# Another order of side work in the first tile of a fused group-norm, mixture-of-experts convolution

## The chip, the cores and the metric

The kernel runs on one core of a Trainium2 chip. The metric is the device time of one execution in microseconds (us), the median of several runs. The lower the better.

## The reference

The input is a batch of 32 images with 384 channels of 28 x 28 pixels (784 per image). Each image is group-normalised (32 groups), passes a layer of 4 experts, and is added to the input:

```python
def _L0_conv_ref(x, gate_w, gate_b, w1, b1, w2, b2):
    scores = jax.nn.softmax(x_flat @ gate_w + gate_b, -1)
    top_v, top_i = jax.lax.top_k(scores, K)          # K = 2
    top_w = jax.nn.softmax(top_v, -1)
    wmap = top_w.T.reshape(K, b, h, w)
    present = (top_i[:, :, None] == jnp.arange(e)[None, None, :]).any(0)
    coef = jnp.einsum('ke,kbhw->ebhw', present.astype(x.dtype), wmap)
    hdn = jax.nn.relu(jnp.einsum('bchw,edc->ebdhw', x, w1) + b1[:, None, :, None, None])
    y = jnp.einsum('ebdhw,eod->ebohw', hdn, w2) + b2[:, None, :, None, None]
    out = jnp.einsum('ebohw,ebhw->bohw', y, coef)
    return out
...
x = x + _L0_conv_ref(_gn(x), ...)
```

Every pixel goes through all four experts (384 to 384 to 384). The gate only weights them: `present` says which experts are first or second choice anywhere in the batch, and `coef` weights each expert at each pixel.

## The kernel before, in words

**Tiling.** The 32 x 784 pixels are cut into 49 tiles of 512. A tile has 12 chunks, one for each expert and each 128 of its 384 hidden units; chunk q runs from 0 to 587. Three chunks (one expert of one tile) are a unit u. Each product is made of three matmuls in a reduced fp32 format, from a rounded part (`_hi`) and a remainder (`_lo`) of both operands. One chunk of the first layer (`mm1`, to `z_ps`) is nine matmuls of 128x512, and one chunk of the second layer (`mm2`, to `y_ps`) is nine too. This text calls either of them a group of nine.

**The pipeline of a chunk.** TensorE (PE) makes z. VectorE (DVE) adds the bias and multiplies by the coefficient (`scale(q)`, output `hid`). ScalarE (ACT) takes the rounded part (`split_h_hi(q)`, `h_hi`). DVE makes the remainder (`split_h_lo(q)`, `h_lo`). PE multiplies by the second weights. `z_ps` has four buffers, so `mm1` of chunk q waits for `scale(q-4)`. PE's order is `mm1` of unit u+1, then `mm2` of unit u.

**Order.** Each engine's program is one list in the order of the code, with semaphores between engines; there is no scheduler. DVE's loop runs over q, and in iteration q it does `scale(q+1)`, then `split_h_lo(q)`, then the side work that is written for this q. If `scale(q+1)` waits, `split_h_lo(q)` stands behind it.

**Side work.** For each image: statistics (`stats` in two halves, `group_stats`), a power on GpSimd (POOL), `norm_columns`, `normalise` in two halves. For each tile: its rounded part and remainder in one or two pieces (`split_x_hi` on ACT, `split_x_lo` on DVE). For each image the gate: `gate_product` on PE (to `g_ps`), `gate_copy` on ACT, `gate_logits` on DVE, `gate_exp` on ACT, `gate_top2` and `gate_gap` on DVE, `gate_gap_exp` on ACT, `gate_weights` and `gate_coefs` on DVE (output `wrow`). SyncE's queue (SP) stores `wrow` to `rows_dram` (`rows_out`) and loads it back over all partitions as `rows` (`rows_in`). `scale` of the first chunk of a tile waits for its `rows`. Tile 0 lies in image 0; tile 1 needs images 0 and 1, so chunk 12 (the first of tile 1) waits for the gate of image 1. For each tile `add_bias` prepares the residual in `res`, and `add_product`, two chunks into the next tile, adds `y_ps` to it and frees `y_ps` for the next tile's `mm2`.

**The start.** Before the loop, PE makes the first eight chunks with `mm1_early` (chunks 0 to 2, 3 to 5, and 6 and 7), ACT rounds the weights (`weight_hi`) and empties the first four z with `relu_early` into `early`, and DVE makes weight remainders (`weight_lo`; `weight_lo(0, 3)` is that of the first layer's fourth expert, used from chunk 9 on). `sum_counts` is the small PE product that sums the counts of the experts' picks. `biases` makes `bias01` and `bias_gap` from 9 tiny DVE instructions; `add_bias` and `add_product` use them.

Of the kernel before, what the change touches and what calls it, by code (L numbers as in the profile page):

```python
# [9 lines left out]
NK = HID // P  # L10
# [16 lines left out]
EARLY = 4  # L27
# [37 lines left out]
def conv_moe(nc, x, gate_w, gate_b, w1, b1, w2, b2, out):  # L65
# [7 lines left out]
    with ctx:  # L73
# [141 lines left out]
        main = Sems("")  # L215
# [171 lines left out]
                                    hi[:, e].rearrange("p j d -> p (j d)").bitcast(f32),  # L387
                                    ALU.subtract).then_inc(ready, 1)

        def mm1_early(pe, u, chunks, terms):  # L390


            for i, term in enumerate(terms):
                if term == "hl":
                    pe.wait_ge(main.xlo_ready, 1)
                if term == "lh":
                    pe.wait_ge(w1lo_ready, u + 1)
                if term == "hh":
                    pe.wait_ge(main.xhi_ready, 1)
                    pe.wait_ge(whi_ready[0], u + 1)  # L400
                for k in chunks:
                    q = NK * u + k
                    if i == 0 and q >= ZB:
                        pe.wait_ge(early_done, q - ZB + 1)
                    ks = slice(k * P, (k + 1) * P)
                    for j in range(NJ):
                        w = (w1_hi, w1_lo)[term[0] == "l"][:, u, j, ks]
                        x = (x_hi, x_lo)[term[1] == "l"][:, 0, j]
                        ins = nc.tensor.matmul(z_ps[:, q % ZB], w, x, start=(i == 0 and j == 0),
                                               stop=(i == 2 and j == NJ - 1))  # L410
                    if i == 2:
                        ins.then_inc(z_ready, 1)

# [134 lines left out]
        def _(dve):  # L548
            lk = Links(dve, dve_step, 0)
# [87 lines left out]
            for q in range(CHUNKS):  # L637
# [3 lines left out]
                if q < CHUNKS - 1:  # L641
                    scale(dve, q + 1)
                split_h_lo(dve, q)
                if r == 4:
                    add_bias(dve, t, lk)
                if q == 0:
                    stats(dve, main, 1, 1, 0, lk)
                if q == 1:
                    stats(dve, main, 1, 1, 1, lk)
                    weight_lo(dve, 0, 3)  # L650
                if q == 2:
                    group_stats(dve, main, 1, lk)
                    biases(lk)
                if q == 3:
                    split_x_lo(dve, 1, 0)
                    norm_columns(dve, main, 1, lk)
                    normalise(dve, main, 1, 1, 0, HALF)
                if q == 4:
                    normalise(dve, main, 1, 1, HALF, PIX)
                if q == 5:  # L660
                    split_x_lo(dve, 1, 1)
                if q == 7:
                    gate_logits(dve, main, 1, lk)
# [3 lines left out]
                if q == 9:  # L667
                    gate_weights(dve, 1, lk)
                    gate_coefs(lk, wrow_ready)
                for n, off in preparing(q):  # L670
                    if off == 0:
                        stats(dve, main, n // SLOTS + (n % SLOTS > 0), n % SLOTS, 0, lk)
                    if off == 1:
                        stats(dve, main, n // SLOTS + (n % SLOTS > 0), n % SLOTS, 1, lk)
                        group_stats(dve, main, n, lk)
                    if off == 3:
                        norm_columns(dve, main, n, lk)
                        normalise(dve, main, n, n % SLOTS, 0, HALF)
                    if off == 4:
                        normalise(dve, main, n, n % SLOTS, HALF, PIX)  # L680
                    if off == 10:
                        gate_logits(dve, main, n, lk)
                    if off == 11:
                        gate_top2(dve, main, n, lk)
                        gate_gap(dve)
                    if off == 13:
                        gate_weights(dve, n, lk)
                        gate_coefs(lk, wrow_ready)
# [6 lines left out]
        def _(act):  # L695
# [12 lines left out]
            act.wait_ge(small_loaded, 48)  # L708
            gate_gap_exp(act, 0)
            weight_hi(1, 0)  # L710
            weight_hi(1, 1)
            relu_early(act, 0)
            weight_hi(1, 2)
            relu_early(act, 1)
            weight_hi(1, 3)
            for q in range(2, EARLY):
                relu_early(act, q)
            split_x_hi(act, 1, 0)
            act.wait_ge(flag_ready, 1)
            flag = act.value_load(missing[0:1, 0:1], min_val=0, max_val=1)  # L720
# [6 lines left out]
            for q in range(CHUNKS):  # L727
                t, r = divmod(q, TILE_CHUNKS)
                split_h_hi(act, q)
                if q == 4:  # L730
                    split_x_hi(act, 1, 1)
                if q == 6:
                    gate_copy(act, main, 1)
                if q == 7:
                    gate_exp(act, main, 1)
                if q == 8:
                    gate_gap_exp(act, 1)
# [87 lines left out]
        def _(pe):  # L825
# [3 lines left out]
                nc.tensor.matmul(g_ps[:, 0:P], ones[:, :], ones[:, :], start=True, stop=True)  # L829
            gate_product(pe, main, 0, 0)  # L830
            mm1_early(pe, 0, range(NK), ("hh", "lh", "hl"))
            sum_counts(pe, main)
            mm1_early(pe, 1, range(NK), ("hh", "hl", "lh"))
            mm1_early(pe, 2, range(2), ("hh", "hl", "lh"))
            pe.wait_ge(flag_ready, 1)
            flag = pe.value_load(missing[0:1, 0:1], min_val=0, max_val=1)
# [3 lines left out]
                sum_counts(pe, scan)  # L840

            for u in range(UNITS):
                if u == 2:
                    gate_product(pe, main, 1, 1)
                for n in range(2, B):
                    if NK * u == TILE_CHUNKS * first_tile(n) - LEAD + 8:
                        gate_product(pe, main, n, n % SLOTS)
                if 0 < u < UNITS - 1:
                    mm1(pe, u + 1, chunks=range(2 if u == 1 else 0, NK))
                mm2(pe, u)  # L850


# [24 lines left out]
```

## Time and profile before

| | |
|---|---|
| median of 3 runs | 2474.2 us (2473.63 to 2474.5) |
| profiled execution | 2474.33 us |
| its span | 2472.5 us |
| PE busy | 2451.0 us, 99% of the span |
| DVE busy | 1414.0 us, 57% |
| ACT busy | 465.4 us, 19% |
| chain that ended last | PE 98%, DVE 2% |

The span is the time between the first and the last recorded instruction; 1.8 us of the profiled execution's time lie outside it. Busy time of PE counts overlapping matmuls once, so idle time can be read as gaps. In a timeline row the columns are the start, the busy time, the engine, the line, the operation with its output and inputs, the count, and in square brackets the idle time of the engine before it with what ended it. A 128x512 matmul has a busy time of 0.39 us, but its successor starts 0.23 us after it, since matmuls are pipelined.

### The profile page before, as it was taken

Reading aid. Unit: us, or ns where it says so; the run is one execution under the profiler, and the core shown is the slowest. Engines: PE = TensorE matmul, PEld = TensorE weight load, DVE = VectorE, ACT = ScalarE, POOL = GpSimd, SP = SyncE. Lnnn points to the kernel's source line nnn. Section 1 sums busy time; section 2 is a strip of 40 time slices with the busy share of each in tenths; the row PEclk is TensorE's granted clock in tenths of the full one; section 3 lists DMA queues with packets and bytes.
Section 4 is the critical chain, followed back from the end, with each engine's and each line's share of the span. In section 5 each row is a group of like instructions: output and inputs, shape, how many; then the busy total and the mean of one; then the engine's idle time right before and its main releaser. Section 6 shows DMA issues by size and latency. Waiting matters only on the chain.

```text
span 2472.5 us, 27781 instructions
## 1 busy us (share of the span) xinstructions
PE 2451.0 (99%) x11372; PEld 2010.6 (81%) x11372; DVE 1414.0 (57%) x2952; ACT 465.4 (19%) x777; POOL 52.6 (2%) x36
## 2 busy tenths in 40 slices
PE   7999999999999999999999999999999999999999
PEld 5888888888888888888888888888888888888887
DVE  8656546556565565645564565546556564555443
ACT  3121111112111111111111121112112111121111
POOL 0000000000000000000000000000000000000000
PEclk9999999999999999999999999999999999999999
DMA  5223121321222113221322123121211222113110
GB/s 184 90 70 114 49 89 58 102 71 49 89 81 81 67 49 108 75 68 47 101 83 68 67 72 112 49 89 67 96 67 49 90 94 68 67 51 106 56 47 26
DMA packets 127520, 189.58 MB, mean 77 GB/s; under 512 B 16032, under 2 KB 80800, under 8 KB 127392
## 3 DMA queue, kind: packets, MB, share of 16 engines
q1 hardware_dynamic: 127392, 187.80, 22.4%
q8 instruction: 89, 1.46, 0.2%
q14 instruction: 39, 0.32, 0.0%
HBM read 146.03 MB, written 41.75 MB: 76 GB/s over the span
## 4 chain that ended last, share of the span: by engine, by line
PE 98%; DVE 2%; DMA 0%; issue 0%; POOL 0%; SPq 0%; ACT 0%; DVEq 0%; POOLq 0%
PE z_ps L430 16%; PE y_ps L449 16%; PE y_ps L451 16%; PE y_ps L450 16%; PE z_ps L432 16%; PE z_ps L431 16%; PE g_ps L300 1%; DVE w_lo L386 0%; DMA x_raw<-in_x 0%; DVE h_lo L488 0%; DVE x_raw L278 0%; DVE st L245 0%; DMA rows_dram<-wrow 0%; DVE hid L477 0%; DVE hid L474 0%
## 5 line engine op out<-in xcount | busy, mean ns | idle before, releaser
L477 DVE SCALAR_TENSOR_TENSOR hid<-z_ps,b_sb,rows 128x512 f32<-128x512 f32 x584 | 436.7, 748 | 901.9 <-PE z_ps L432 894.5
L449 PE MATMUL y_ps<-h_lo,w_hi 128*128 128x512 f32 x1764 | 687.2, 390 | 4.3 <-DVE h_lo L488 4.3
L451 PE MATMUL y_ps<-h_hi,w_hi 128*128 128x512 f32 x1764 | 686.9, 389 | 0.0
L450 PE MATMUL y_ps<-h_hi,w_lo 128*128 128x512 f32 x1764 | 686.8, 389 | 0.0
L430 PE MATMUL z_ps<-x_lo,w_hi 128*128 128x512 f32 x1740 | 680.9, 391 | 2.2 <-DVE hid L477 2.2
L432 PE MATMUL z_ps<-x_hi,w_hi 128*128 128x512 f32 x1740 | 677.4, 389 | 0.0
L431 PE MATMUL z_ps<-x_hi,w_lo 128*128 128x512 f32 x1740 | 676.8, 389 | 0.0
L484 ACT ACTIVATE h_hi<-hid 128x512 fp32r<-128x512 f32 x588 | 368.5, 631 | 1562.3 <-DVE hid L477 1553.4
L488 DVE SCALAR_TENSOR_TENSOR h_lo<-hid,h_hi 128x512 fp32r<-128x512 f32 x588 | 401.1, 682 | 8.3 <-ACT h_hi L484 7.1
L449 PEld LDWEIGHTS y_ps<-h_lo,w_hi 128*128 128x128 f32 x1764 | 331.5, 188 | 74.8 <-DVE h_lo L488 5.3
L430 PEld LDWEIGHTS z_ps<-x_lo,w_hi 128*128 128x128 f32 x1740 | 326.6, 188 | 78.8 <-issue 12.3
L451 PEld LDWEIGHTS y_ps<-h_hi,w_hi 128*128 128x128 f32 x1764 | 331.5, 188 | 68.8
L450 PEld LDWEIGHTS y_ps<-h_hi,w_lo 128*128 128x128 f32 x1764 | 331.5, 188 | 68.7
L432 PEld LDWEIGHTS z_ps<-x_hi,w_hi 128*128 128x128 f32 x1740 | 326.7, 188 | 68.5
L431 PEld LDWEIGHTS z_ps<-x_hi,w_lo 128*128 128x128 f32 x1740 | 326.7, 188 | 67.1
L506 DVE SCALAR_TENSOR_TENSOR res<-y_ps,bias,res 128x512 f32<-128x512 f32 x147 | 101.1, 743 | 111.5 <-PE y_ps L451 111.5
L495 DVE SCALAR_TENSOR_TENSOR res<-rows,bias_gap,res 128x512 f32<-128x512 f32 x147 | 101.5, 746 | 0.0
L267 POOL TENSOR_TENSOR rstd<-gvar_eps,minus_half 128x8 f32<-128x8 f32 x32 | 52.4, 1638 | 2221.8 <-DVE gvar_eps L262 2221.8
L245 DVE BATCH_NORM_STATS2 st<-x_raw 128x6 f32<-128x392 f32 x186 | 92.4, 552 | 0.0
L292 DVE TENSOR_TENSOR x_lo<-x_raw,x_hi 128x1536 fp32r<-128x1536 f32 (+31 forms) x80 | 90.3, 1129 | 0.0
L286 ACT CAST x_hi<-x_raw 128x1536 fp32r<-128x1536 f32 (+31 forms) x80 | 77.1, 964 | 5.0 <-DVE x_raw L278 5.0
L278 DVE TENSOR_SCALAR x_raw<-x_raw,norm 128x1176 f32<-128x1176 f32 (+1 forms) x64 | 69.9, 1093 | 1.2
(88 smaller groups left out, 374.4 us busy)
## 6 DMA issues: line engine op xcount, KB each, us to landing
rows<-rows_dram SPq DMA_DIRECT2D x48, 1280.0 KB, 6.1
x_raw<-in_x SPq DMA_DIRECT2D x62, 588.0 KB, 5.9
res<-in_x SPq DMA_DIRECT2D x18, 768.0 KB, 5.6
out<-res SPq DMA_DIRECT2D x17, 768.0 KB, 4.3
rows_dram<-wrow SPq DMA_DIRECT2D x32, 98.0 KB
w_in<-in_w SPq DMA_DIRECT2D x3, 576.0 KB, 10.2
res<-in_x SPq DMA_DIRECT2D x2, 744.0 KB, 4.9
out<-res SPq DMA_DIRECT2D x2, 744.0 KB, 4.1
```

The lines of the kernel that those rows point to most:

```text
L245: ins = nc.vector.bn_stats(st6[:, HALVES * j + h], x_raw[:, q, j, half(h)])
L430: nc.tensor.matmul(z, w1_hi[:, e, j, ks], lo, start=(j == 0), stop=False)
L431: nc.tensor.matmul(z, w1_lo[:, e, j, ks], hi, start=False, stop=False)
L432: ins = nc.tensor.matmul(z, w1_hi[:, e, j, ks], hi, start=False, stop=(j == NJ - 1))
L449: nc.tensor.matmul(y, w2_hi[:, e, k, ms], h_lo[:, slot], start=first, stop=False)
L450: nc.tensor.matmul(y, w2_lo[:, e, k, ms], h_hi[:, slot], start=False, stop=False)
L451: ins = nc.tensor.matmul(y, w2_hi[:, e, k, ms], h_hi[:, slot], start=False, stop=last)
L477: nc.vector.scalar_tensor_tensor(hid[:, q % HIDS], z_ps[:, q % ZB], b1_sb[:, e, k:k + 1], coef, ALU.add, ALU.mult).then_inc(scaled, 1)
L484: nc.scalar.activation(h_hi[:, q % RING], hid[:, q % HIDS], ACT.Relu).then_inc(hhi_ready, 1)
L488: nc.vector.scalar_tensor_tensor(h_lo[:, q % RING], hid[:, q % HIDS], 0.0, h_hi[:, q % RING].bitcast(f32), ALU.max, ALU.subtract).then_inc ...
L495: lk.inc(nc.vector.scalar_tensor_tensor(xs, rows[:, t % 2, E], bias_gap[:, m:m + 1], xs, ALU.mult, ALU.add))
L506: nc.vector.scalar_tensor_tensor(xs, y_ps[:, m], bias01[:, 1, m:m + 1], xs, ALU.add, ALU.add).then_inc(out_ready, 1)
```

## The change

Only the order of instructions changes. In DVE's loop, the second image's statistics move from iterations 0 and 1 to 2 and 3, `weight_lo(0, 3)` from 1 to 4, `group_stats` from 2 to 5, `split_x_lo(1, 0)` from 3 to 5, `norm_columns` and both halves of `normalise` to 6, and `split_x_lo(1, 1)` to 6 as well. `biases` (from iteration 2) and `add_bias` of tile 0 (from iteration 4) move to the end of iteration 9, behind `gate_coefs`. ACT empties chunks 0 to 2 before it rounds three more weights, and its gate steps move by a chunk. On PE, `sum_counts` moves behind the first three matmuls of `mm1_early(1)`, and the gate product of image 1 moves behind `mm1` of unit 3.

```diff
-        def mm1_early(pe, u, chunks, terms):
+        def mm1_early(pe, u, chunks, terms, counts=False):
...
+                    if counts and i == 0 and k == 0:
+                        sum_counts(pe, main)
...
                 split_h_lo(dve, q)
-                if r == 4:
+                if r == 4 and t:
                     add_bias(dve, t, lk)
-                if q == 0:
+                if q == 2:
                     stats(dve, main, 1, 1, 0, lk)
-                if q == 1:
+                if q == 3:
                     stats(dve, main, 1, 1, 1, lk)
+                if q == 4:
                     weight_lo(dve, 0, 3)
-                if q == 2:
+                if q == 5:
                     group_stats(dve, main, 1, lk)
-                    biases(lk)
-                if q == 3:
                     split_x_lo(dve, 1, 0)
+                if q == 6:
                     norm_columns(dve, main, 1, lk)
                     normalise(dve, main, 1, 1, 0, HALF)
-                if q == 4:
                     normalise(dve, main, 1, 1, HALF, PIX)
-                if q == 5:
                     split_x_lo(dve, 1, 1)
...
                     gate_coefs(lk, wrow_ready)
+                    biases(lk)
+                    add_bias(dve, 0, lk)
...
             weight_hi(1, 0)
+            for q in range(3):
+                relu_early(act, q)
             weight_hi(1, 1)
-            relu_early(act, 0)
             weight_hi(1, 2)
-            relu_early(act, 1)
+            relu_early(act, 3)
             weight_hi(1, 3)
-            for q in range(2, EARLY):
-                relu_early(act, q)
             split_x_hi(act, 1, 0)
...
                 split_h_hi(act, q)
-                if q == 4:
+                if q == 6:
                     split_x_hi(act, 1, 1)
-                if q == 6:
+                if q == 7:
                     gate_copy(act, main, 1)
-                if q == 7:
                     gate_exp(act, main, 1)
...
-            sum_counts(pe, main)
-            mm1_early(pe, 1, range(NK), ("hh", "hl", "lh"))
+            mm1_early(pe, 1, range(NK), ("hh", "hl", "lh"), counts=True)
...
             for u in range(UNITS):
-                if u == 2:
-                    gate_product(pe, main, 1, 1)
...
                     mm1(pe, u + 1, chunks=range(2 if u == 1 else 0, NK))
+                if u == 2:
+                    gate_product(pe, main, 1, 1)
                 mm2(pe, u)
```

DVE from chunk 1 on, before (`hid` is `scale`, `h_lo` is `split_h_lo`, `st` the statistics, `w_lo` the weight remainder):

```order
L474 TENSOR_TENSOR hid<-rows 128x512 x2
L488 SCALAR_TENSOR_TENSOR h_lo<-hid,h_hi 128x512
L245 BN_STATS st<-x_raw 128x6 x3
L474 TENSOR_TENSOR hid<-rows 128x512
L488 SCALAR_TENSOR_TENSOR h_lo<-hid,h_hi 128x512
L245 BN_STATS st<-x_raw 128x6 x3
L386 TENSOR_TENSOR w_lo<-w_in,w_hi 128x1152
L474 TENSOR_TENSOR hid<-rows 128x512
L488 SCALAR_TENSOR_TENSOR h_lo<-hid,h_hi 128x512
```

And DVE at the same place of the changed kernel:

```order
L476 TENSOR_TENSOR hid<-rows 128x512 x2
L490 SCALAR_TENSOR_TENSOR h_lo<-hid,h_hi 128x512
L476 TENSOR_TENSOR hid<-rows 128x512
L490 SCALAR_TENSOR_TENSOR h_lo<-hid,h_hi 128x512
L476 TENSOR_TENSOR hid<-rows 128x512
L490 SCALAR_TENSOR_TENSOR h_lo<-hid,h_hi 128x512
L245 BN_STATS st<-x_raw 128x6 x3
L479 SCALAR_TENSOR_TENSOR hid<-z_ps,b_sb,rows 128x512
L490 SCALAR_TENSOR_TENSOR h_lo<-hid,h_hi 128x512
L245 BN_STATS st<-x_raw 128x6 x3
```

The remainders of chunks 1 and 2 no longer stand behind statistics and the weight remainder.

DVE at the end of iteration 9 and in iteration 10, before (`wrow` is the end of the gate of image 1):

```order
L357 TENSOR_TENSOR wpix<-wpix,wtmp 128x7x4
L358 STREAM_TRANSPOSE wrow<-wpix 128x224
L477 SCALAR_TENSOR_TENSOR hid<-z_ps,b_sb,rows 128x512
L488 SCALAR_TENSOR_TENSOR h_lo<-hid,h_hi 128x512
L245 BN_STATS st<-x_raw 128x6 x3
```

And in the changed kernel:

```order
L357 TENSOR_TENSOR wpix<-wpix,wtmp 128x7x4
L358 STREAM_TRANSPOSE wrow<-wpix 128x224
L628 TENSOR_SCALAR bias<-b_sb,present 128x3 x2
L633 SCALAR_TENSOR_TENSOR bias<-b_sb,present,bias 128x3 x6
L637 TENSOR_TENSOR bias_gap<-bias 128x3
L497 SCALAR_TENSOR_TENSOR res<-rows,bias_gap,res 128x512 x3
L479 SCALAR_TENSOR_TENSOR hid<-z_ps,b_sb,rows 128x512
L490 SCALAR_TENSOR_TENSOR h_lo<-hid,h_hi 128x512
L245 BN_STATS st<-x_raw 128x6 x3
```

Twelve instructions now stand between the gate of image 1 and `scale(11)`.

PE around the gate product of image 1, before (`g_ps` is the gate product; the rows ahead of it end `mm2` of unit 1, the rows behind it begin `mm1` of unit 3):

```order
L449 MATMUL y_ps<-h_lo,w_hi 128x512
L450 MATMUL y_ps<-h_hi,w_lo 128x512
L451 MATMUL y_ps<-h_hi,w_hi 128x512
L300 MATMUL g_ps<-x_raw,gw_pad 32x196 x12
L430 MATMUL z_ps<-x_lo,w_hi 128x512
L431 MATMUL z_ps<-x_hi,w_lo 128x512
L432 MATMUL z_ps<-x_hi,w_hi 128x512
```

And in the changed kernel, where the rows ahead of it end `mm1` of unit 3 and the rows behind it begin `mm2` of unit 2:

```order
L432 MATMUL z_ps<-x_lo,w_hi 128x512
L433 MATMUL z_ps<-x_hi,w_lo 128x512
L434 MATMUL z_ps<-x_hi,w_hi 128x512
L300 MATMUL g_ps<-x_raw,gw_pad 32x196 x12
L451 MATMUL y_ps<-h_lo,w_hi 128x512
L452 MATMUL y_ps<-h_hi,w_lo 128x512
L453 MATMUL y_ps<-h_hi,w_hi 128x512
```

The product stands three groups of nine later in PE's list.

## Rows read from the trace of the kernel before

**Rows 1.** The page: busy time and share of the span.

```profile
PE 2451.0 (99%) x11372; PEld 2010.6 (81%) x11372; DVE 1414.0 (57%) x2952; ACT 465.4 (19%) x777; POOL 52.6 (2%) x36
```

**Rows 2.** Windows: busy time and count of each engine, PE's clock, DMA.

```profile
50.00:60.00 10.00, 8.09 (x46) 5.44 (x46) 6.95 (x10) 1.35 (x4) 0.00 (x0) 0.83 0.01 2
...
56.00:58.00 2.00, 2.00 (x5) 1.07 (x4) 0.95 (x2) 0.00 (x0) 0.00 (x0) 0.50 0.00 0
```

**Rows 3.** Timeline of PE from the first `mm2` on.

```profile
34.79 0.47 PE L449 MATMUL y_ps<-h_lo,w_hi 128*128 128x512 f32 x1 [0.63 <-DVE h_lo L488]
...
41.19 0.50 PE L449 MATMUL y_ps<-h_lo,w_hi 128*128 128x512 f32 x1 [1.54 <-DVE h_lo L488]
...
45.75 0.47 PE L430 MATMUL z_ps<-x_lo,w_hi 128*128 128x512 f32 x1 [2.23 <-DVE hid L477]
...
54.26 0.50 PE L449 MATMUL y_ps<-h_lo,w_hi 128*128 128x512 f32 x1 [1.91 <-DVE h_lo L488]
...
58.01 1.26 PE L300 MATMUL g_ps<-x_raw,gw_pad 128*32 128x196 f32 x24
...
77.72 0.39 PE L449 MATMUL y_ps<-h_lo,w_hi 128*128 128x512 f32 x1
...
81.80 0.39 PE L449 MATMUL y_ps<-h_lo,w_hi 128*128 128x512 f32 x1
```

**Rows 4.** Timeline of PE during `mm1_early`.

```profile
25.02 0.97 PE L409 MATMUL z_ps<-x_hi,w_hi 128*128 128x512 f32 x3 [0.58 <-ACT rows L459]
...
32.64 1.52 PE L409 MATMUL z_ps<-x_hi,w_lo 128*128 128x512 f32 x6
```

**Rows 5.** Timeline of ACT during `mm1_early`.

```profile
21.61 1.15 ACT L699 CAST w_hi<-hid 128x1152 fp32r<-128x1152 f32 x1
22.66 0.68 ACT L459 ACTIVATE rows<-z_ps,b_sb 128x512 f32<-128x512 f32 x1
```

**Rows 6.** Timeline of DVE, chunks 0 to 6.

```profile
32.56 1.29 DVE L474 TENSOR_TENSOR hid<-rows 128x512 f32<-128x512 f32 x2 [0.50 <-DVE w_lo L386]
...
34.56 1.50 DVE L245 BATCH_NORM_STATS2 st<-x_raw 128x6 f32<-128x392 f32 x3
...
43.09 0.35 DVE L626 TENSOR_SCALAR bias<-b_sb,present 128x3 f32<-128x3 f32 x2
...
44.85 0.75 DVE L477 SCALAR_TENSOR_TENSOR hid<-z_ps,b_sb,rows 128x512 f32<-128x512 f32 x1
...
46.12 1.00 DVE L292 TENSOR_TENSOR x_lo<-x_raw,x_hi 128x816 fp32r<-128x816 f32 x1
...
49.87 2.07 DVE L495 SCALAR_TENSOR_TENSOR res<-rows,bias_gap,res 128x512 f32<-128x512 f32 x3
...
52.87 0.74 DVE L477 SCALAR_TENSOR_TENSOR hid<-z_ps,b_sb,rows 128x512 f32<-128x512 f32 x1
```

**Rows 7.** Timeline of ACT, gate of image 1.

```profile
59.35 0.32 ACT L307 COPY lg_rows<-g_ps 128x196 f32<-128x196 f32 x1 [5.02 <-PE g_ps L300]
...
62.07 0.62 ACT L484 ACTIVATE h_hi<-hid 128x512 fp32r<-128x512 f32 x1
```

**Rows 8.** Timeline of DVE, gate of image 1 to `add_product` of tile 0.

```profile
60.84 0.40 DVE L317 STREAM_TRANSPOSE lg_pix<-lg_rows 128x224 f32<-128x224 f32 x1
...
62.72 0.69 DVE L488 SCALAR_TENSOR_TENSOR h_lo<-hid,h_hi 128x512 fp32r<-128x512 f32 x1 [0.15 <-ACT h_hi L484]
...
77.67 0.75 DVE L477 SCALAR_TENSOR_TENSOR hid<-z_ps,b_sb,rows 128x512 f32<-128x512 f32 x1 [7.01 <-DMA rows<-rows_dram]
...
86.62 2.05 DVE L506 SCALAR_TENSOR_TENSOR res<-y_ps,bias,res 128x512 f32<-128x512 f32 x3
```

**Rows 9.** Timeline of SP's queue: the load of `rows` for tile 1.

```profile
71.15 0.94 SPq L529 DMA_DIRECT2D rows<-rows_dram  x2
```

**Rows 10.** The page's DMA issues: count, KB each, median us to landing.

```profile
rows<-rows_dram SPq DMA_DIRECT2D x48, 1280.0 KB, 6.1
```

**Rows 11.** Timeline of PE: a gate product at full clock.

```profile
108.41 1.20 PE L300 MATMUL g_ps<-x_raw,gw_pad 128*32 128x196 f32 x24
```

## The prediction

> **What bounds the kernel now.** I read the page first: PE is busy 99% of the span [rows 1], so over the whole run only PE's work, its clock and its few gaps count. Windows of ten microseconds then show that every one from 60 us on has PE busy throughout at full clock; the one from 50 to 60 us has 8.09 us busy and a mean clock of 0.83, and inside it the stretch from 56 to 58 us ran at 0.50, that is 1.2 instead of 2.4 GHz [rows 2]. So what can be gained lies in the first 60 us. The timeline of PE gives it one by one: from the start of `mm2` of chunk 0 at 34.79 us PE waits 1.54 us for the remainder of chunk 2, 2.23 us for `scale(4)`, and 1.91 us for the remainder of chunk 5 [rows 3]. After the last wait the clock falls, and a group of nine takes 3.75 us (54.26 to 58.01) where one at full clock takes 2.04 (two groups from 77.72 to 81.80) [rows 3]. DVE is late, not PE: side work of image 1 and of the biases stands between the chunks that PE waits for. Before 34.79 us PE waits 0.58 us for `relu_early` [rows 4], but that costs nothing, since `mm2` of chunk 0 waits for `scale(0)` at 32.56 [rows 6], which waits for DVE's weight remainders and the row of coefficients.
>
> **The early part.** In `mm1_early`, `relu_early(0)` takes the place of a cast and starts at 21.61 instead of 22.66 us [rows 5]; the other two follow at once. PE then doesn't wait at 25.02, `sum_counts` moves by a tenth and DVE takes its result later anyway, and PE's early work ends some 1.6 us sooner: 32.4 instead of 34.0 us (32.64 plus six matmuls) [rows 4]. DVE's list up to `scale(0)` is untouched and every cast that it needs is there (the last weight cast moves to about 27.8, DVE wants it at 30.7). So `mm2` of chunk 0 still begins at 34.79: worth 0, and PE's gap ahead of it grows from 0.63 to about 2.4 us. That matters only for the clock.
>
> **DVE to the gate product.** A pair of `scale` and `split_h_lo` costs DVE 1.27 us (44.85 to 46.12) [rows 6], less than PE's 2.04 for a group. Without the statistics (1.42 us) behind chunk 0, the remainders of chunks 1 and 2 are done at 35.8 and 37.0, where PE wants them at 36.9 and 39.0. Two statistics, the weight remainder and the group statistics then stand behind pairs that PE has not asked for. The closest of these dates is the remainder of chunk 1, with 1.1 us to spare; the fourth expert's weight remainder is done at 43.6 and wanted at 49.1. Chunk 5's remainder, the one that is late now, is done near 45 and wanted at 47.1. For the second `normalise` I shift a row: it ends by 52.87 now [rows 6]. The change takes `biases` (43.09 to 44.85, 1.76 us) and `add_bias` (49.87 to the next start, 1.99 us) from in front of it and puts two pairs there (2.5 us): about 51.6. The three waits vanish.
>
> **PE to the same point.** From 34.79, ten groups of nine (`mm2` of units 0 and 1, the last chunk of `mm1` of unit 2, `mm1` of unit 3) at 2.04 and 0.1 for the slower first matmul (0.47 against 0.39) [rows 3] end at 55.3. By then `normalise` is done, so the gate product doesn't wait; it takes 1.2 us [rows 11] and ends at 56.5. Had it stayed in front of `mm1` of unit 3 it would have stood at 49.1 and waited 2.5 us. Six more groups bring PE to 68.75, the start of `mm2` of unit 3, which is at 77.72 now; its third group could start at 72.85 instead of 81.80 [rows 3]. Up to here 8.95 us are won: the waits of 5.7, some 1.6 of slow clock, the rest in small gaps and restarts.
>
> **What is late next.** The gate product moved three groups (6.1 us) towards its consumers on PE. Behind it runs a chain of fixed length: copy (0.32) [rows 7], logits to the next rounded part 60.84 to 62.07 (1.23), 0.65 to the remainder of chunk 8 at 62.72 [rows 7, 8]. With the copy at 56.51 this remainder starts at 58.74, 3.98 us sooner than now. From it to the load of `rows` the instructions are the same, one for one, so the load is issued at 71.15 - 3.98 = 67.17 [rows 9]. `biases` and `add_bias` now follow (3.75 us on DVE), then `scale(11)`, the remainder of chunk 10 and a statistic: DVE is free again at about 70.5, still ahead of the load, in a wait that is 7.01 us now [rows 8]. That cover makes the moved 3.75 us cost nothing; without it they would delay `scale(11)`. The load took 6.5 us (71.15 to 77.65, before `scale(12)` at 77.67) [rows 8, 9]; the median of 48 is 6.1 [rows 10]. The load for tile 2 now sits 0.5 us behind it; it will come 1.3 us behind, because it waits for `scale(11)`. I take 6.3, landing at 73.5.
>
> Behind `scale(12)`, which waits for this landing, stands the remainder of chunk 11. It is done 1.35 us later (0.75 and 0.69 less their overlap) and PE starts 0.05 after that: 74.9. PE is there at 72.85. **So a new wait of about 2.05 us appears**, in front of the third group of `mm2` of unit 3, and 0.1 for the restart. Now PE gets there at 81.80 with the remainder done at 79.0, so the present order has 2.8 us to spare. The next consumer is `add_product` of tile 0, 8.95 us behind `scale(12)` on DVE (77.67 to 86.62) [rows 8]: first `y_ps` free at 83.2, wanted by PE at 74.9 + 0.1 + 4 x 2.04 = 83.2. A tie; I charge 0.1. After that DVE needs less than PE for each chunk and nothing else is near. Sum without the clock: 81.80 - 74.9 - 0.1 - 0.1 = 6.7 us faster.
>
> For the load, the sum hangs on whether the transfer behind slows the one ahead. The rows show 6.5 with one close behind and 6.1 as a median. The Trainium skill (DMA: Bandwidth & Descriptors, Queues, rings and completion order) says that each DMA engine takes up the descriptors of one issuing queue in ring order. By that rule sending the second load later gains nothing for the first, and the sum would be 6.5 instead of 6.7. This trace can't tell which.
>
> **The clock.** Of the three waits of over 1.5 us, 1.54, 2.23 and 1.91, only the last was followed by the half clock [rows 2, 3]. The changed kernel has two gaps of that kind, about 2.4 us ahead of 34.79 and 2.05 ahead of 74.9, and PE sets the end behind both, so a slow stretch costs its full price: 3.75 - 2.14 = 1.6 us for the one in the trace. I expect one slow stretch, at 1.5 us, since one may fall partly into the gap. If the first gap brings it, everything moves by 1.5 and the second gap falls elsewhere. Result: 6.7 - 1.5 = 5.2 us, from 2474.33 (the profiled execution, 0.1 above the median of the runs) to 2469.1.
>
> **Rivals.** (1) No slow stretch: 2474.3 - 6.7 = 2467.6. For it: two of three such waits had none. The Trainium skill (TensorE: Matmul & The Clock Gate, Part 1) says that the moment of a clock change varies from run to run because the gate's own timing doesn't start with the kernel; by that, the runs of both kernels would scatter between these cases. (2) Two slow stretches: 2474.3 - 6.7 + 3.2 = 2470.8. For it: both gaps are longer than the 1.91 that was followed by one. (3) The change does not do what it says: DVE's work between the early chunks is not what PE waits for, or another wait (the coefficients of experts 1 to 3, needed by `scale(3)` from 35.7 on) takes its place, and less than 2 us are won: 2472.5 to 2474. The pair at 1.27 speaks against it. (4) Slower: the load of `rows` lands late. It is now the last link before PE; each microsecond of it goes straight to the end. It must take over 13 us instead of 6.3 to eat up 6.7. No load of `rows` in this trace is near that, though bulk loads beside it in the queue could do it.
>
> **Chances.** Forecast (one slow stretch) 0.50, none 0.25, two 0.15, rival 3 0.07, slower 0.03. What a measurement of this kernel can tell from no change is about 0.2%, 4.9 us, so 2469.25 is the border, and the likeliest case lies almost on it. Faster by more: all of the 0.25, and somewhat over half of the 0.50, 0.55 in all; within 0.2%: 0.42; slower: 0.03. The range leaves out the last two cases: from 2467.0 (no slow stretch and a load of 5.9) to 2471.2 (two, and a load of 6.7).
>
> **What would show it.** In the changed kernel's PE timeline: a gap of 2.2 to 2.4 us ahead of the first `mm2`, still near 34.8; no wait from there to the gate product near 55.3; one wait near 72.8 of about 2 us for the remainder of chunk 11; `scale(12)` waiting for `rows` by 2 to 3 us; `biases` and `add_bias` inside the former wait. Each slow stretch moves the later dates by 1.6. The prediction is wrong if the wait at chunk 11 is missing or longer than 3 us, if the gate product waits for `normalise`, or if PE's gap ahead of 34.8 is followed by a slow clock that lasts longer than the one seen.

## The result, and the profile after

The changed kernel runs in 2468.97 us (median of 17 runs, 2467.69 to 2470.57) against 2473.63 us for the kernel before (17 runs, 2472.45 to 2475.23). The ratio is 0.9981, with a 95% interval of 0.9974 to 0.9989: 4.7 us or 0.19% faster. The profiled execution took 2469.91 us, 4.4 less than that of the kernel before. One of the 19 runs of the kernel before whose median stands as 2472.88 in the first table below took 3092.3 us, at a mean granted clock of 0.748, and is left out.

In the windows of the changed kernel (columns as in [rows 2]: the stretch, its length, busy time and count of PE, PE's weight loads, DVE, ACT and POOL, PE's granted clock, DMA share, GB/s) the gaps stand elsewhere than before:

```profile
30.00:40.00 10.00, 7.89 (x28) 6.13 (x27) 9.49 (x15) 3.13 (x5) 0.00 (x0) 0.83 0.94 329
34.90:38.20 3.30, 3.25 (x8) 2.63 (x9) 3.30 (x7) 1.26 (x2) 0.00 (x0) 0.50 1.03 372
40.00:50.00 10.00, 10.00 (x46) 8.27 (x45) 9.51 (x24) 1.26 (x2) 2.33 (x1) 1.00 0.26 82
50.00:60.00 10.00, 10.00 (x64) 7.76 (x63) 5.36 (x11) 1.81 (x5) 0.00 (x0) 1.00 0.00 0
70.00:80.00 10.00, 7.89 (x35) 6.20 (x34) 6.49 (x18) 1.26 (x2) 0.00 (x0) 1.00 0.79 264
```

From 40 to 60 us, where [rows 3] have waits of 2.23 and 1.91 us and a slow stretch, PE is busy throughout. There are two gaps of 2.1 us, one ahead of 35 us and one ahead of 77 us, and the stretch at half clock (a slow stretch, in what follows) now comes with the first. That first gap costs nothing by itself: PE is only done with its early work sooner, and the first `mm2` starts at 34.95 where it stood at 34.79.

The timeline of PE, the rows that answer to [rows 3] and [rows 11]:

```profile
34.95 0.77 PE L451 MATMUL y_ps<-h_lo,w_hi 128*128 128x512 f32 x1 [2.10 <-DVE h_lo L490]
35.52 0.63 PE L452 MATMUL y_ps<-h_hi,w_lo 128*128 128x512 f32 x1
...
38.40 0.39 PE L453 MATMUL y_ps<-h_hi,w_hi 128*128 128x512 f32 x1
...
57.11 1.20 PE L300 MATMUL g_ps<-x_raw,gw_pad 128*32 128x196 f32 x24
58.24 0.50 PE L451 MATMUL y_ps<-h_lo,w_hi 128*128 128x512 f32 x1
...
76.97 0.50 PE L451 MATMUL y_ps<-h_lo,w_hi 128*128 128x512 f32 x1 [2.10 <-DVE h_lo L490]
...
85.42 0.47 PE L451 MATMUL y_ps<-h_lo,w_hi 128*128 128x512 f32 x1
```

The row at 76.97 is the third group of `mm2` of unit 3, at 81.80 in [rows 3]. The two waits in brackets are the only ones from 30 to 100 us, and only between 34.95 and 38.40 do matmuls in a row take over 0.6 us. A single first matmul behind a wait or behind the gate product takes 0.47 or 0.50. The row at 85.42 is the first matmul of tile 1 into `y_ps`: it follows its predecessor (85.08) by 0.34 us instead of 0.23, the restart of an engine that has just been held up.

DVE and SP around the gate of image 1, answering to [rows 8, 9], in the timeline of the changed kernel:

```profile
58.73 0.41 DVE L317 STREAM_TRANSPOSE lg_pix<-lg_rows 128x224 f32<-128x224 f32 x1 [4.50 <-ACT lg_rows L307]
...
60.62 0.69 DVE L490 SCALAR_TENSOR_TENSOR h_lo<-hid,h_hi 128x512 fp32r<-128x512 f32 x1 [0.16 <-ACT h_hi L486]
...
67.56 2.08 DVE L497 SCALAR_TENSOR_TENSOR res<-rows,bias_gap,res 128x512 f32<-128x512 f32 x3
...
75.57 0.75 DVE L479 SCALAR_TENSOR_TENSOR hid<-z_ps,b_sb,rows 128x512 f32<-128x512 f32 x1 [3.26 <-DMA rows<-rows_dram]
76.24 0.68 DVE L490 SCALAR_TENSOR_TENSOR h_lo<-hid,h_hi 128x512 fp32r<-128x512 f32 x1
...
84.54 2.05 DVE L508 SCALAR_TENSOR_TENSOR res<-y_ps,bias,res 128x512 f32<-128x512 f32 x3
```

```profile
69.06 1.68 SPq L531 DMA_DIRECT2D rows<-rows_dram  x2
```

`scale(12)` waits for `rows` and the remainder of chunk 11 stands behind it; PE takes that up at 76.97, 0.05 us after its end. `add_bias` (67.56) lies inside the former wait of 7.01 us, of which 3.26 are left.

### The profile page after: what moved, and what is told of

The parts are those of the page before. It is cut to its first block, busy times and chain, and to the rows that moved or that the text cites. A ratio compares the mean times of both kernels' runs of the same rounds, so it can differ in the third digit from the quotient of the medians.

```text
span 2468.1 us, 27782 instructions
## 1 busy us (share of the span) xinstructions
PE 2449.9 (99%) x11372; PEld 2011.4 (81%) x11372; DVE 1413.7 (57%) x2952; ACT 465.6 (19%) x777; POOL 53.3 (2%) x36
## 4 chain that ended last, share of the span: by engine, by line
PE 98%; DVE 1%; DMA 1%; issue 0%; ACT 0%; POOL 0%; SPq 0%; DVEq 0%; POOLq 0%
PE z_ps L432 16%; PE y_ps L451 16%; PE y_ps L452 16%; PE y_ps L453 16%; PE z_ps L434 16%; PE z_ps L433 16%; PE g_ps L300 1%; DMA rows<-rows_dram 0%; DMA rows_dram<-wrow 0%; DMA x_raw<-in_x 0%; DVE w_lo L386 0%; DVE h_lo L490 0%; DVE x_raw L278 0%; ACT h_hi L486 0%; POOL rstd L267 0%
```

## The experiments

Each kernel was timed beside the kernel before on the same chip, and what can be compared between chips is the difference of the two medians. The 95% intervals of the ratios reach 0.0009 to 0.0012 to either side, 2 to 3 us, so the medians alone do not settle a difference of 1 or 2 us between two variants. The timelines and the second table below do that. For each run the mean granted clock of the whole run is also known, to three digits. A stretch of 3.4 us at half clock takes about 0.0007 from it, so runs given as 0.999 have such a stretch besides the idle end of the run, and runs given as 1.000 have none. In all 13 profiled executions this reading holds. The last column counts runs with such a stretch.

| kernel | median, us | before on its chip | difference | range | with a slow stretch |
|---|---|---|---|---|---|
| changed | 2468.97 | 2473.63 | -4.66 | 2467.69 to 2470.57 | 7 of 17 |
| changed, again | 2468.40 | 2472.88 | -4.48 | 2467.69 to 2470.25 | 4 of 11 |
| without the early part | 2469.61 | 2473.48 | -3.87 | 2467.71 to 2470.17 | 7 of 11 |
| early part alone | 2473.40 | 2473.48 | -0.08 | 2472.44 to 2475.18 | 10 of 11 |
| gate product first | 2468.91 | 2473.48 | -4.57 | 2467.95 to 2470.47 | 6 of 11 |
| gate product in the middle | 2467.11 | 2473.48 | -6.37 | 2465.57 to 2468.72 | 5 of 10 |
| chunk 11 ahead of `scale(12)` | 2467.16 | 2473.44 | -6.28 | 2465.50 to 2468.19 | 8 of 10 |
| gap filled | 2469.38 | 2473.44 | -4.06 | 2467.70 to 2470.10 | 7 of 11 |
| biases in their old place | 2471.21 | 2473.44 | -2.23 | 2469.63 to 2472.82 | 11 of 11 |
| biases moved alone | 2469.05 | 2473.44 | -4.39 | 2468.46 to 2469.71 | 0 of 11 |
| combination | 2465.36 | 2472.88 | -7.52 | 2464.69 to 2466.04 | 0 of 7 |
| chunk 11 first, gap filled | 2465.60 | 2472.88 | -7.28 | 2464.99 to 2466.17 | 0 of 7 |

The profiled executions can be compared more closely. Their first `mm2` starts between 34.0 and 35.6 us, and the table splits the time of each at that start, which takes the scatter of the start out of the comparison. From the start of `mm2` of unit 7 to the end, all 13 take 2346.27 to 2346.31 us: whatever tells the kernels apart lies in the first 130 us.

| kernel | time of the profiled execution | first `mm2` starts | from there to the end | its slow stretch comes with |
|---|---|---|---|---|
| before | 2474.33 | 34.79 | 2439.54 | the wait of 1.91 at chunk 5 |
| early part alone | 2474.72 | 35.16 | 2439.56 | the wait of 1.91 at chunk 5 |
| biases in their old place | 2470.53 | 34.03 | 2436.50 | the wait of 2.19 at chunk 11 |
| gate product first | 2469.77 | 34.70 | 2435.07 | the wait of 2.68 at the gate product |
| changed | 2469.91 | 34.95 | 2434.96 | the gap of 2.10 ahead of the first `mm2` |
| without the early part | 2469.61 | 34.85 | 2434.76 | the wait of 2.14 at chunk 11 |
| biases moved alone | 2468.46 | 34.21 | 2434.25 | none |
| changed, again | 2467.69 | 34.21 | 2433.48 | none |
| gap filled | 2468.84 | 35.55 | 2433.29 | none |
| chunk 11 ahead of `scale(12)` | 2466.87 | 34.52 | 2432.35 | the gap of 2.22 ahead of the first `mm2` |
| gate product in the middle | 2466.43 | 35.04 | 2431.39 | none |
| chunk 11 first, gap filled | 2464.99 | 34.25 | 2430.74 | none |
| combination | 2465.39 | 34.69 | 2430.70 | none |

**Without the early part.** ACT's early order and `sum_counts` as before, all else as in the changed kernel.

```diff
             weight_hi(1, 0)
-            for q in range(3):
-                relu_early(act, q)
             weight_hi(1, 1)
+            relu_early(act, 0)
             weight_hi(1, 2)
-            relu_early(act, 3)
+            relu_early(act, 1)
             weight_hi(1, 3)
+            for q in range(2, EARLY):
+                relu_early(act, q)
...
-            mm1_early(pe, 1, range(NK), ("hh", "hl", "lh"), counts=True)
+            sum_counts(pe, main)
+            mm1_early(pe, 1, range(NK), ("hh", "hl", "lh"))
```

> The changed kernel with ACT's early order and the place of sum_counts as before; only the side work in the loop and the gate product stay moved. Theory 1 (the gain is DVE's side work moved away from chunks 1 to 5, and a new wait at chunk 11 is what is left): the early part is worth nothing, PE's gap ahead of the first mm2 shrinks from 2.1 to about 0.6 us and brings no slow stretch, so all runs should lie near the fast ones of the changed kernel, median about 2468.3 us. The wait of about 2.1 us at chunk 11 stays and may still bring a slow stretch. Theory 2 (the early part carries a share of the gain, since PE ends its early work 1.6 us sooner): 1 to 1.6 us slower than the changed kernel, about 2470.3.

Measured 2469.61, between the theories by the median. The timeline of PE decides:

```profile
34.85 0.47 PE L451 MATMUL y_ps<-h_lo,w_hi 128*128 128x512 f32 x1 [0.75 <-DVE h_lo L490]
...
75.35 0.50 PE L451 MATMUL y_ps<-h_lo,w_hi 128*128 128x512 f32 x1 [2.14 <-DVE h_lo L490]
```

The first `mm2` starts at the same time, 34.85 instead of 34.95, though PE ended its early work later. So the early part gains nothing: from that start to the end the profiled execution takes 2434.76 us, against 2434.96 for the changed kernel, each with one slow stretch. The four runs without a slow stretch have a median of 2468.29, the expected value. In the profiled execution, one of the other seven, the stretch comes with the wait at chunk 11 (76 to 79 us, mean clock 0.54); where it lies in the remaining six is not recorded. I had put too little weight on that second gap.

**The early part alone.** The reverse edit of the diff above, made to the kernel before.

> The kernel before with only ACT's early order and the place of sum_counts changed. Theory 1: nothing gained, 2473 to 2474.5 us, first mm2 near 34.8 with a gap of 2.1 us ahead of it; the three waits of 1.5 to 2.2 us remain, and a slow stretch behind the longer first gap is hidden in them. Theory 2: 1 to 1.6 us faster, about 2472.3.

Measured 2473.40, 0.08 below the kernel before. The medians leave room for 2 us; the timeline makes theory 2 fall, since the first `mm2` does not start sooner and the time from there to the end is the same (2439.56 against 2439.54).

```profile
35.16 0.47 PE L451 MATMUL y_ps<-h_lo,w_hi 128*128 128x512 f32 x1 [2.47 <-DVE h_lo L490]
...
41.56 0.50 PE L451 MATMUL y_ps<-h_lo,w_hi 128*128 128x512 f32 x1 [1.54 <-DVE h_lo L490]
46.11 0.47 PE L432 MATMUL z_ps<-x_lo,w_hi 128*128 128x512 f32 x1 [2.19 <-DVE hid L479]
54.61 0.74 PE L451 MATMUL y_ps<-h_lo,w_hi 128*128 128x512 f32 x1 [1.91 <-DVE h_lo L490]
```

The gap ahead of the first `mm2` has grown from 0.63 to 2.47 us and the three waits stand as before. The slow stretch of this execution does not come with the gap of 2.47 but, as in the kernel before, with the wait of 1.91.

**Gate product first.** Its old place, ahead of `mm1` of unit 3, in the changed kernel.

```diff
             for u in range(UNITS):
+                if u == 2:
+                    gate_product(pe, main, 1, 1)
...
                     mm1(pe, u + 1, chunks=range(2 if u == 1 else 0, NK))
-                if u == 2:
-                    gate_product(pe, main, 1, 1)
```

> The changed kernel with the gate product of image 1 in its old place on PE, ahead of mm1 of unit 3. Theory 1: PE waits there for the second normalise, from 49.1 to about 52.1, so 2.5 to 3 us at full clock (1.4 less behind a slow stretch); in exchange the rows land some 3 us sooner against PE and the wait at chunk 11 is gone. Sum: from 0.3 us faster to 0.8 slower than the changed kernel, 2468.2 to 2469.8. Rival (the place of the gate product is what wins): back near 2472.

Measured 2468.91, as the changed kernel. PE waits for `normalise` instead of for chunk 11:

```profile
51.95 1.20 PE L300 MATMUL g_ps<-x_raw,gw_pad 128*32 128x196 f32 x24 [2.68 <-DVE x_raw L278]
```

No other wait follows. The move of the gate product behind `mm1` thus traded a wait of 2.7 us for one of 2.1, and from the first `mm2` to the end the two take the same time (2435.07 and 2434.96).

**Gate product in the middle**, behind the second of the three chunks of `mm1` of unit 3.

```diff
-                if 0 < u < UNITS - 1:
-                    mm1(pe, u + 1, chunks=range(2 if u == 1 else 0, NK))
                 if u == 2:
+                    mm1(pe, u + 1, chunks=range(0, 2))
                     gate_product(pe, main, 1, 1)
+                    mm1(pe, u + 1, chunks=range(2, NK))
+                elif 0 < u < UNITS - 1:
+                    mm1(pe, u + 1, chunks=range(2 if u == 1 else 0, NK))
                 mm2(pe, u)
```

> The changed kernel with the gate product behind the second of three chunks of mm1 of unit 3. Theory 1: the product starts at 53.3 with normalise done at 52.1, no wait; its chain ends 2.04 us sooner against PE, so the wait at chunk 11 falls from 2.1 to 0.1 us or less, and 2.0 us are gained: median about 2466.9. Rival (the wait at chunk 11 is covered or returns elsewhere, for example at y_ps behind add_product): no gain, 2469.

Measured 2467.11; 1.7 us more are gained than by the changed kernel. In the list of PE's waits from 33 to 100 us one is left, ahead of the first `mm2`:

```profile
PE y_ps L451 <- DVE h_lo L490: 1.7, 1, 1.7
```

**Chunk 11 ahead of `scale(12)`** on DVE, in the changed kernel.

```diff
-                if q < CHUNKS - 1:
+                if q < CHUNKS - 1 and q != TILE_CHUNKS - 1:
                     scale(dve, q + 1)
                 split_h_lo(dve, q)
...
                         group_stats(dve, main, n, lk)
+                    if off == 1 and q == TILE_CHUNKS - 1:
+                        scale(dve, q + 1)
```

> The changed kernel with DVE's scale(12), which waits for rows, moved behind the remainder of chunk 11 and the statistics of image 2, which need no rows. Theory 1: the wait at chunk 11 is gone (2.1 us), add_product of tile 0 comes 3 us sooner against the landing and so isn't the next wait; 2.1 us and the restart gained: median about 2466.8. Rival: the wait moves on to y_ps or to scale(12) and under 0.5 us are gained.

Measured 2467.16, 1.6 us more than the changed kernel gains. No wait of PE is left from 60 us on. DVE now fills the wait for `rows` with the remainder and the statistics, and `add_product` starts at 80.97 where the changed kernel has 84.54:

```profile
71.86 0.67 DVE L490 SCALAR_TENSOR_TENSOR h_lo<-hid,h_hi 128x512 fp32r<-128x512 f32 x1
72.46 1.49 DVE L245 BATCH_NORM_STATS2 st<-x_raw 128x6 f32<-128x392 f32 x3
...
76.06 1.41 DVE L479 SCALAR_TENSOR_TENSOR hid<-z_ps,b_sb,rows 128x512 f32<-128x512 f32 x2
...
80.97 2.05 DVE L508 SCALAR_TENSOR_TENSOR res<-y_ps,bias,res 128x512 f32<-128x512 f32 x3
```

These two kernels remove the same wait, of 2.1 us, from either side: one lets the rows land sooner, the other no longer makes chunk 11 wait for them. By the medians it was worth 1.7 and 1.6 us, but the shares of runs with a slow stretch differ (7 of 17 for the changed kernel, 5 of 10 and 8 of 10 here). Profiled executions of the same kind, from the first `mm2` to the end, give 2.1 us for the gate product in the middle (2431.39 against 2433.48, both without a stretch) and 2.6 for chunk 11 ahead of `scale(12)` (2432.35 against 2434.96, both with one).

**Gap filled.** Nine extra matmuls ahead of the loop, in the changed kernel.

```diff
+            for _ in range(9):
+                nc.tensor.matmul(g_ps[:, :], w1_hi[:, 0, 0, 0:P], x_hi[:, 0, 0], start=True, stop=True)
             for u in range(UNITS):
```

> The changed kernel with nine extra 128x512 matmuls on PE in the gap ahead of the first mm2 (their result is not used). Clock theory: the two groups of runs, near 2468.4 and 2470.3, differ by a slow stretch behind this gap, which 2 us of matmuls close; runs then lie near 2468.4 and only the wait at chunk 11 can still bring a slow stretch. Rival (the scatter comes from the start of the run or from DMA): two groups as before, or 0.1 to 0.5 us slower for the extra work.

Measured 2469.38, with a slow stretch in 7 of 11 runs. The profiled execution has no wait ahead of the first `mm2` and one of 2.13 us at chunk 11. The filling was somewhat long there: the first `mm2` starts at 35.55, 0.5 us after its remainder is done. This run decided nothing: the kernel with the second gap alone has slow stretches in no smaller share of its runs than the one with both.

**Biases in their old place**, all else as in the changed kernel.

```diff
-                if r == 4 and t:
+                if r == 4:
                     add_bias(dve, t, lk)
                 if q == 2:
                     stats(dve, main, 1, 1, 0, lk)
+                    biases(lk)
...
                     gate_coefs(lk, wrow_ready)
-                    biases(lk)
-                    add_bias(dve, 0, lk)
```

> The changed kernel with biases back in iteration 2 and add_bias of tile 0 back in iteration 4. Theory 1: 1.76 and 1.99 us return to DVE ahead of chunk 5, whose remainder is then done near 48.7 and wanted at 47.1 at full clock: a wait of 1.6 us, and the second normalise ends near 55.8 instead of 52.1, 0.5 late for the gate product. 1.6 to 2.1 us slower than the changed kernel, about 2470.8, less in runs with a slow stretch behind the first gap. Rival (the statistics were the whole matter, biases are hidden): no change, 2469.

Measured 2471.21, half of the gain lost. The wait for chunk 5 is back, smaller, and those ahead of the first `mm2` (1.75) and at chunk 11 (2.19) are still there; the gate product does not wait:

```profile
47.97 0.50 PE L451 MATMUL y_ps<-h_lo,w_hi 128*128 128x512 f32 x1 [1.31 <-DVE h_lo L490]
```

From the first `mm2` to the end this is 1.5 us more than in the changed kernel (2436.50 against 2434.96, one slow stretch each). The median moved by more, since all 11 runs have a stretch here.

**Biases moved alone**, to the kernel before.

```diff
-                if r == 4:
+                if r == 4 and t:
                     add_bias(dve, t, lk)
...
                     group_stats(dve, main, 1, lk)
-                    biases(lk)
...
                     gate_coefs(lk, wrow_ready)
+                    biases(lk)
+                    add_bias(dve, 0, lk)
```

> The kernel before with only biases and add_bias of tile 0 moved behind gate_coefs in iteration 9. Theory 1: the wait of 2.23 us for scale(4) falls by 1.76 and that of 1.91 for chunk 5 by the 1.99 of add_bias, or vanishes; the gate product keeps its early place, so the wait at chunk 11 does not arise (2.8 us to spare less what PE gains, but the whole gate chain moves with it). 3.5 to 4 us faster than before, and without a wait of 1.9 us no slow stretch there: 2469.5 to 2470. Rival (the order of statistics is the matter): under 1.5 us faster, 2472.5.

Measured 2469.05: by the median these two moves alone give what the whole change gives. The waits that are left, in PE's timeline:

```profile
36.72 0.50 PE L449 MATMUL y_ps<-h_lo,w_hi 128*128 128x512 f32 x1 [0.20 <-DVE h_lo L488]
...
40.60 0.50 PE L449 MATMUL y_ps<-h_lo,w_hi 128*128 128x512 f32 x1 [1.54 <-DVE h_lo L488]
...
43.41 0.47 PE L430 MATMUL z_ps<-x_lo,w_hi 128*128 128x512 f32 x1 [0.46 <-DVE hid L477]
...
52.20 1.20 PE L300 MATMUL g_ps<-x_raw,gw_pad 128*32 128x196 f32 x24
```

The 2.23 of [rows 3] has lost the 1.76 of `biases` and is 0.46; the 1.91 ahead of chunk 5 is gone; the 1.54 stands. The gate product comes early and there is no wait at chunk 11. None of the 11 runs has a slow stretch, and their range is 1.25 us wide instead of 2.9.

**The combination**: ACT's early order as before, the gate product in the middle, and chunk 11 ahead of `scale(12)`, by the three diffs above.

> The version made of the parts that won: the side work moved as in the changed kernel, ACT's early order as before, the gate product behind the second chunk of mm1 of unit 3, and scale(12) behind the remainder of chunk 11. Theory 1: no wait of PE over 1 us is left behind its early work, so each run is like the best ones of the last two variants: median about 2466.2 us and a scatter of about 1.3 us, since no gap is left that a slow stretch could follow. Rival (the two edits remove the same wait and the scatter has another source): median 2467.1 with a scatter of 3 us.

**Chunk 11 first, gap filled**: the two diffs above together.

> The variant with scale(12) behind the remainder of chunk 11, and nine extra 128x512 matmuls on PE in the gap ahead of the first mm2 (their result is not used). That variant has one gap of 2 us left, this one closes it. Clock theory: no slow stretch in any run, median about 2466.2 us, scatter about 1.3 us instead of 2.7. Rival: median 2467.2 and the same scatter.

**The changed kernel again.**

> The changed kernel again, unaltered, beside the two others on one chip. Both theories: median 2468.5 to 2469.5, in two groups near 2468.4 and 2470.3.

Measured 2468.40: 7 runs without a slow stretch (median 2468.28) and 4 with one (2470.07), as expected. Its profiled execution has both gaps and no stretch:

```profile
34.21 0.47 PE L451 MATMUL y_ps<-h_lo,w_hi 128*128 128x512 f32 x1 [2.16 <-DVE h_lo L490]
...
74.78 0.50 PE L451 MATMUL y_ps<-h_lo,w_hi 128*128 128x512 f32 x1 [2.23 <-DVE h_lo L490]
```

The combination took 2465.36 us, 7.5 less than the kernel before beside it (ratio 0.9970, 0.9958 to 0.9981) and 3.0 less than the changed kernel beside it. With the second of the three (2465.60, the same within the scatter) it is the fastest version of this study. Of the 0.8 by which it undercuts its expectation, 0.6 is the kernel before, which was that much lower on this chip. In the list of PE's waits from 30 to 100 us one is left:

```profile
PE y_ps L451 <- DVE h_lo L490: 0.8, 1, 0.8
```

The second kernel, chunk 11 first with the gap filled, is to be read against the one without the extra matmuls (on another chip):

```profile
34.52 0.74 PE L451 MATMUL y_ps<-h_lo,w_hi 128*128 128x512 f32 x1 [2.22 <-DVE h_lo L490]
```

And filled:

```profile
34.25 0.47 PE L451 MATMUL y_ps<-h_lo,w_hi 128*128 128x512 f32 x1 [0.32 <-DVE h_lo L490]
```

Without the extra matmuls 8 of 10 runs had a slow stretch and the range was 2.7 us; with them none of 7, and 1.2 us. The only difference in the programs is that PE works in the gap instead of idling, so here the clock theory holds: the gap brings the slow stretch. A range of 1.2 us is left without any stretch, and 1.25 and 1.35 in the two other kernels that have none. In the profiled executions the start of the first `mm2` alone differs by 1.1 us (34.03 to 35.16, the filled gap at 35.55 aside), while the time behind it agrees to 0.02 us between the kernel before and the early part alone, and to 0.04 between the two last rows of the table. So the scatter of the changed kernel has two parts: when the first `mm2` starts, and whether a stretch comes.

## Why the prediction was right

**The three waits and what they cost.** As forecast, they vanish. What the prediction did not separate is which move does it. Moving `biases` and `add_bias` alone gives 4.4 us by the medians, and 5.3 between the profiled executions from the first `mm2` on (2439.54 less 2434.25: 1.91 and 1.77 of waits and the slow stretch). The moves of the statistics and the weight remainder remove the remaining 2.2 us of waits (0.20, 1.54 and 0.46), but the longer run of DVE work delays `normalise` against PE, and that returns 2.1 us at chunk 11 or 2.7 at the gate product. What they add on top is 0.8 us in an execution without a slow stretch (2434.25 less 2433.48), nothing by the median, and 3.5 us once that wait is removed too, as in the combination (2434.25 less 2430.70).

**The early part at 0.** Right, in both directions (without it, and alone). Its gap of 2.1 us (2.16 when run again) was forecast at 2.4.

**Dates.** The gate product was forecast at 55.3 plus 1.5 for a slow stretch and stands at 57.11. Of the 0.3 between, 0.16 is the later start of the first `mm2`; the rest is the stretch, which cost 1.58 by then (counted from the first `mm2`, the product starts at 22.16 here and at 20.58 in the execution without a stretch), and 0.06 in PE's list. PE was forecast to be ready for chunk 11 at 72.85 plus 1.5 and was at 74.87 (76.97 less 2.10): 0.2 more was lost between the gate product and chunk 11. Part of it is the first matmul behind the product, which takes 0.50 instead of 0.39; the sum had nothing for it.

**The new wait.** Forecast 2.05 us for the remainder of chunk 11, measured 2.10 (2.23 when run again). Gate chain, load and `scale(12)` went as worked out: from the start of the gate product to the remainder of chunk 8, 3.51 us against 3.43 (58.74 less 55.31). `scale(12)` waited 3.26 us for `rows`, forecast 2 to 3.

**The load.** I took 6.3 us between the 6.5 of the row and the 6.1 of the median. It landed by 75.57, 6.5 us after its issue at 69.06. In the ten profiled executions where `scale(12)` waits for it, this takes 6.51 to 6.65 us, whether the next load is issued 0.5 us behind it or 1.3. So sending the next load later gave it nothing, which fits the Trainium skill's rule that descriptors are taken up in ring order (DMA: Bandwidth & Descriptors, Queues, rings and completion order). The sum by that rule and the row was the better choice than mine, by 0.2 us.

**The tie at `y_ps`.** Forecast within 0.1 us of each other: `add_product` began at 84.54, its first part ended near 85.3, and PE restarted at 85.42 with 0.1 lost.

**The clock.** I forecast one slow stretch at 1.5 us as the usual case. The price was right: the two profiled executions of the changed kernel, one with a stretch and one without, differ by 1.5 us from the first `mm2` to the end (2434.96 and 2433.48). Between groups of runs the price is less sharp: 2.0 us in the 17 runs (10 without a stretch, median 2468.44, and 7 with one, 2470.41), and 1.1 to 1.8 in the six other sets of the changed kernel and its variants that have runs of both kinds. The chance was wrong: having no stretch is likelier, and I gave it 0.25.

**The sum without the clock** was too large. From the first `mm2` on, the kernel before takes 2439.54 us and the changed kernel without a stretch 2433.48: 6.1 us are gained, and 6.7 were forecast. Of the 0.6, 0.3 is PE's date at chunk 11 and 0.2 the load. So without a stretch I forecast 2467.6, and the runs without one have a median of 2468.44.

**What is luck.** The forecast of 2469.1 lies between the two groups, at a value that few single runs have, and the close hit of the median is partly luck. The sum also started from a profiled execution of 2474.33 us, and the median of the kernel before turned out to be 0.7 lower; that offset made up for the gain that was put too high. As a gain, 5.2 was forecast and 4.7 measured.

**What stays open.** The runs of the kernel before nearly all have a slow stretch (28 of 32 in the first set), yet they spread over 2.9 us too, of which the start of the first `mm2` may account for 1.1. Its few runs without a stretch are hardly faster than the others: medians of 2473.21 (4 runs) against 2473.51 in the first set. So the 1.6 us that the stretch costs in its profiled execution is not what it costs that kernel as a rule. A stretch behind the wait for `scale(4)` would be hidden in the wait for chunk 5, and one behind chunk 5 would not. That would give two values from one stretch, but no profile of one of that kernel's shorter runs was taken, so this is argued and not shown.

## What to carry to other kernels

When a few instructions stand between a waiting engine and its input, ask first for the ones that nobody waits for (here `biases` and `add_bias`, 3.75 us) and move them into the next long wait of their own engine; alone they gave as much as the whole change. When a producer of a long chain is moved later, as the gate product was, add up the chain to its last consumer: the 2 us came back there. An instruction that waits for a DMA should not stand in front of one that doesn't. And where medians scatter by more than the difference in question, compare profiled executions from an event that both have to the end: here that agreed to 0.04 us between kernels without a difference behind that event.

## What the runs showed of the hardware

A gap of PE of about 2 us, in a run that was otherwise busy, was enough to bring a stretch at half clock, but not always. With the gaps as the profiled executions show them, the counts are:

| gaps of PE from the first `mm2`'s on, us | kernel | runs with a stretch |
|---|---|---|
| 2.10 and 2.10 (again: 2.16 and 2.23) | changed | 11 of 28 |
| 1.47 and 2.68 | gate product first | 6 of 11 |
| 1.75, 1.31 and 2.19 | biases in their old place | 11 of 11 |
| 2.22 | chunk 11 ahead of `scale(12)` | 8 of 10 |
| 0.75 and 2.14 | without the early part | 7 of 11 |
| 2.13 | gap filled | 7 of 11 |
| 1.67 | gate product in the middle | 5 of 10 |
| 0.54, 0.20, 1.54 and 0.46 | biases moved alone | 0 of 11 |
| 0.76, or 0.32 | combination; chunk 11 first, gap filled | 0 of 14 |

The first gap is not the same in every run: in the six profiled executions of kernels with the changed kernel's early part and no filling it is 1.47 to 2.22 us. Its size does not decide alone: 2.23 and 2.47 us were passed without a stretch in executions where 1.91 brought one, and one kernel went both ways on the same chip. In all seven profiled executions that have a stretch it lasts 3.4 us. It came with the first gap in one profile (34.9 us) and with the one at chunk 11 in another (76 us). This fits the Trainium skill (TensorE: Matmul & The Clock Gate, Part 1), which has the clock gate's timing run on its own, so that the moment of a change varies from run to run. For a comparison of less than 0.1% it means that a median over such runs measures how often the clock fell as well as the change.
